# Batch 0 projected head by head into its stacked rows, and the second span's groups spread two to a step, in a one-core language-model layer

## The chip, the cores and the metric

One Trainium2 chip, and of it one core. The time is that of one execution on the device, in microseconds (us), and the number that counts is the median of several executions. All engines of the core run at once: PE (matrix products), DVE (vector work), ACT (activations, copies), POOL (general vector work and, here, the indirect DMAs), and SP, which only issues DMAs. Each engine takes its instructions strictly in order; semaphores tie them together.

## What is computed

Four thousand and ninety-six tokens, in 8 batches of 512, go through three layers. Layer norm and attention are per batch; nothing of one batch's attention depends on another's.

```python
h = einsum('bsd,bsde->bse', base_embeddings[ids], rule_transform[token_rules[ids]])   # D = 64, 100 rules
n = layernorm(h)
q, k = einsum('btd,hrd->bhtr', n, Q), einsum('bud,hrd->bhur', n, K)                  # 8 heads, R = 32
attn = softmax(einsum('bhtr,bhur->bhtu', q, k) / 8)
h = h + einsum('bhtd,hde->bte', einsum('bhtu,bud->bhtd', attn, n), VO)
f = layernorm(h)
y = sum over the top 2 of 8 experts of weight * (relu(f @ W1[e] + b1[e]) @ W2[e] + b2[e])
out = h + y
```

All of it is float32. Products that need the precision are made from two halves, a high part (fp32r) and what is left over (the low part).

## The kernel before

**Spans and groups.** The product of a token with its rule's 64x64 matrix is made after the tokens have been sorted by rule. The tokens are sorted in two spans: span 0 is batches 0 and 1, span 1 is batches 2 to 7. A sorted span is cut into tiles of 64 rows, each of one rule, and 8 tiles are a *group*: 15 groups in span 0, 19 in span 1. For a group PE transposes the input (line 933, tile `eT`), makes 8 pairs of small products with the rule's matrix (line 942), and an engine copies the result to `y_out`, from where a DMA stores it. POOL then gathers each batch's rows back into token order, 4 indirect DMAs per batch (line 450, `hbuf`). The sorting itself (counts by PE, lines 902 and 903; slots by DVE, lines 688 to 701; scatters by POOL, line 442) comes before a span's groups. For groups that are not among the first 100 rules PE must load the rule's column offset from memory into registers first (`columns`).

**Steps.** From batch 0 on the program is one list of steps (b, k), b from -2 to 8 and k from 0 to 15; all engines walk the same list. A step of PE holds, in this order: two transposed score tiles for the exponentials (line 1041, 97 rows: 96 of data and one of maxima), one score tile for the row maxima (line 1057, 96 rows), the product of the exponentials with the values (line 1069, 4 matmuls, "PV"), a list of auxiliary work (`aux_at`), and the other score tile. The maxima (`mx`, line 849) are made on DVE. A *pair* is two score tiles; pair j belongs to PV step j and is scored 12 steps earlier (`LEAD`). The auxiliary work is the projection of later batches, the expert layer of earlier ones, and, until batch 0 ends, the groups of span 1. It takes the two banks 6 and 7 in turn.

**From layer norm to scores.** `xT` transposes a batch's normed rows (`xs`), four projection parts (`proj`, lines 992 and 993) make q and k for all heads, ACT casts them (`qk_h`) and DVE makes the low part (`qk_l`, line 872). Heads lie in the wrong partitions there, so 24 DMAs of 128 KB each copy them into the stacked tiles `qs` and `ks` (lines 385 and 388), six to each of four head pairs. The scores of a head pair wait for its semaphore `stack_g`. The maxima come back as two half rows per batch: PE transposes them (line 1018), ACT negates them (`negm`), SP copies them into row 96 of `qs` (line 394) and waits for the landing. SP also fetches the softmax sums (`srow`, line 405) in the same queue.

**Where things stand in the list.** Span 1's groups stand at (-1,14), (-1,15) and then three to a step from (0,0) on. Batch 2's `xT` is at (0,13), its projection at (0,14) and (0,15); batch 3's `xT` at (1,4) and its projection at (1,5) to (1,8). All 24 gathers of batches 2 to 7 stand in one row on POOL behind the last group's store. Span 1's counts are made by PE between groups 8 and 14 of span 0. Batch 0's key copies go out on ACT's queue, the rest on SP's.

## Time and profile before

| | us |
|---|---|
| three executions | 675.84, 678.07, 680.62; median 678.07 |
| the profiled execution | 675.75, its span 673.9 |
| PE busy | 525.9 (78% of the span) |
| DVE busy | 409.6 (61%) |
| ACT busy | 285.6 (42%) |
| POOL busy | 238.1 (35%) |

The span is the time between the first and the last instruction. "Idle before, releaser" is the time an engine stood, and what let it go on. "Granted clock" is TensorE's: 1.00 is full speed (2.4 GHz), 0.50 is half (1.2 GHz). A wait put down to "remote" or "another core or an unknown queue" is one whose releaser the trace doesn't name.

### The profile page before, as it was taken

Reading aid. Unit: us, or ns where it says so; the run is one execution under the profiler, and the core shown is the slowest. Engines: PE = TensorE matmul, PEld = TensorE weight load, DVE = VectorE, ACT = ScalarE, POOL = GpSimd, SP = SyncE. Lnnn points to the kernel's source line nnn. Section 1 sums busy time; section 2 is a strip of 40 time slices with the busy share of each in tenths; the row PEclk is TensorE's granted clock in tenths of the full one; section 3 lists DMA queues with packets and bytes.
Section 4 is the critical chain, followed back from the end, with each engine's and each line's share of the span. In section 5 each row is a group of like instructions: output and inputs, shape, how many; then the busy total and the mean of one; then the engine's idle time right before and its main releaser. Section 6 shows DMA issues by size and latency. Waiting matters only on the chain.

```text
span 673.9 us, 9098 instructions
## 1 busy us (share of the span) xinstructions
PE 525.9 (78%) x2604; PEld 278.8 (41%) x2604; DVE 409.6 (61%) x970; ACT 285.6 (42%) x548; POOL 238.1 (35%) x395
## 2 busy tenths in 40 slices
PE   0174903797787296999999999999999999988580
PEld 0043802255452133444544544544554454437240
DVE  5621685662225284788868959868857767446521
ACT  0101301055562153546555555565555465652350
POOL 5674057633237500220333224124133232236414
PEclk9985965579998598999999999999999999995976
DMA  8732414722751035440440440431332000000000
GB/s 245 257 89 57 118 36 92 181 62 71 174 141 26 19 78 114 94 96 4 92 96 1 95 103 1 95 79 26 71 79 48 2 9 2 9 1 9 0 9 8
DMA packets 21774, 47.03 MB, mean 70 GB/s; under 512 B 6240, under 2 KB 11552, under 8 KB 21664
## 3 DMA queue, kind: packets, MB, share of 16 engines
q1 hardware_dynamic: 15392, 32.23, 20.2%
q0 software_dynamic: 4752, 8.20, 4.7%
q10 hardware_dynamic: 1584, 6.03, 2.7%
q8 instruction: 24, 0.39, 0.2%
q14 instruction: 22, 0.18, 0.1%
HBM read 9.97 MB, written 11.01 MB: 31 GB/s over the span
## 4 chain that ended last, share of the span: by engine, by line
PE 58%; DVE 16%; issue 10%; ACT 3%; DMA 3%; another core or an unknown queue 3%; POOL 2%; SPq 2%; POOLq 0%; DVEq 0%; ACTq 0%
PE bank L1069 15%; PE bank L1057 10%; PE bank L1041 8%; PE bank L942 6%; PE bank L1027 5%; DVE mx L849 4%; PE bank L1008 4%; PE bank L1002 2%; PE bank L1003 2%; DVE r_sb L867 2%; POOL r_sb L503 2%; DMA front<-in_weights 1%; PE bank L933 1%; PE bank L988 1%
## 5 line engine op out<-in xcount | busy, mean ns | idle before, releaser
L849 DVE TENSOR_REDUCE mx<-bank 128x1 f32<-128x512 f32 x256 | 171.1, 688 | 107.3 <-PE bank L1057 79.0
L503 POOL TENSOR_TENSOR r_sb<-r_sb 128x256 f32<-128x256 f32 (+2 forms) x192 | 99.7, 519 | 287.9 <-DVE r_sb L884 188.1
L560 ACT ACTIVATE prob<-bank 128x512 f32<-128x512 f32 x256 | 138.9, 596 | 68.8 <-PE bank L1041 50.5
L1069 PE MATMUL bank<-prob,xa 128*64 128x512 f32 x512 | 141.5, 631 | 3.6 <-issue 3.6
L1057 PE MATMUL bank<-ks,qs 96*128 96x512 f32 x256 | 123.2, 487 | 25.7 <-DVE mx L849 21.4
L1057 PEld LDWEIGHTS bank<-ks,qs 96*128 96x128 f32 x256 | 50.9, 199 | 144.7 <-issue 122.5
L1041 PE MATMUL bank<-qs,ks 97*128 97x512 f32 x256 | 89.1, 430 | 0.7 <-DMA qs<-negm 0.4
L600 ACT ACTIVATE r_sb<-bank,stay 128x512 f32<-128x512 f32 x64 | 43.1, 687 | 68.3 <-PE bank L1003 68.2
L1041 PEld LDWEIGHTS bank<-qs,ks 97*128 97x128 f32 x256 | 44.0, 195 | 19.4 <-issue 13.0
L942 PE MATMUL bank<-r_sb,eT 128*64 128x64 f32 (+1 forms) x544 | 43.2, 239 | 10.2 <-ACT eT L543 6.8
L942 PEld LDWEIGHTS bank<-r_sb,eT 128*64 128x64 f32 x544 | 38.4, 151 | 17.8 <-issue 9.2
L1069 PEld LDWEIGHTS bank<-prob,xa 128*64 128x64 f32 x512 | 25.7, 137 | 48.5 <-issue 45.7
L450 POOL DMA_INDIRECT hbuf<-y_sorted,pos x32 | 30.6, 957 | 40.1 <-DMA y_sorted<-y_out 31.0
L442 POOL DMA_INDIRECT emb_sorted<-ctxT,pos x32 | 32.7, 1021 | 12.7 <-issue 12.7
L1027 PEld LDWEIGHTS bank<-stay,ctxT 128*128 128x128 f32 x256 | 34.3, 200 | 6.7 <-issue 2.4
L1027 PE MATMUL bank<-stay,ctxT 128*128 128x128 f32 x256 | 36.2, 287 | 0.3 <-DVE r_sb L884 0.3
L434 POOL DMA_INDIRECT ctxT<-in_table,ids x32 | 31.5, 985 | 13.8 <-issue 9.4
L884 DVE TENSOR_TENSOR r_sb<-bank,rsum 128x512 f32<-128x512 f32 x32 | 22.1, 690 | 21.2 <-PE bank L1027 21.0
L1008 PE MATMUL bank<-r_sb,stay 128*64 128x512 f32 x128 | 32.1, 610 | 2.4 <-ACT r_sb L600 2.4
L606 ACT CAST qk_h<-bank 128x512 fp32r<-128x512 f32 x32 | 18.4, 588 | 31.8 <-PE bank L993 24.8
L1002 PE MATMUL bank<-xs,w_h 128*128 128x512 f32 x64 | 30.8, 481 | 1.0 <-DVE r_sb L884 0.5
L872 DVE TENSOR_TENSOR qk_l<-bank,qk_h 128x512 fp32r<-128x512 f32 x32 | 21.7, 687 | 16.2 <-ACT qk_h L606 13.1
(137 smaller groups left out, 603.3 us busy)
## 6 DMA issues: line engine op xcount, KB each, us to landing
qs<-qk_h SPq DMA_DIRECT2D x64, 128.0 KB
ks<-qk_h SPq DMA_DIRECT2D x56, 128.0 KB
qs<-qk_l SPq DMA_DIRECT2D x32, 128.0 KB
ks<-qk_l SPq DMA_DIRECT2D x28, 128.0 KB
emb_sorted<-front ACTq DMA_DIRECT2D x4, 608.0 KB
y_sorted<-y_out POOLq DMA_DIRECT2D x19, 128.0 KB, 2.5
e_in<-emb_sorted POOLq DMA_DIRECT2D x9, 256.0 KB, 3.0
emb_sorted<-front ACTq DMA_DIRECT2D x3, 640.0 KB
```

Source lines behind the costliest of these rows:

```text
L442: nc.gpsimd.indirect_dma_start(emb_sorted[i], bass.IndirectOffsetOnAxis(ap=pos[:, c:c + 1], axis=0), etok[:, c, 0:D], None).then_inc(S[f"s ...
L503: nc.gpsimd.tensor_tensor(a[:, at:at + width], src[:, 0:width], src[:, width:2 * width], ALU.add).then_inc(S["pool_chain"], 1)
L560: nc.scalar.activation(prob[:, step % NPROB, u % 2, :], bank[u % NST][:], ACT.Exp, scale=SC).then_inc(S["exp_done"], 1)
L600: nc.scalar.activation(hid[:, i, :], ring(a)[:], ACT.Relu, bias=b1_f[:, i:i + 1]).then_inc(S["relu_done"], 1)
L849: V.tensor_reduce(mx[:, u // 16, u % 16:u % 16 + 1], bank[3 + n % 2][:], AX.X, ALU.max).then_inc(S["mx_done"], 1)
L942: last = M(out_[0:TS, s * D:(s + 1) * D], eT[:, g % 2, col:col + TS], r_sb[:, at_:at_ + D] if isinstance(at_, int) else r_sb[:, bass.ds(at ...
L1002: M(out_[:], w1_h[:, i * HID:(i + 1) * HID], xs[:, 1, :], start=True, stop=False)
L1008: last = M(out_[64 * t:64 * t + 64, :], w2_f[:, 2 * i + t, :], hid[:, 2 * i + t, :], start=True, stop=True)
L1027: last = M(out_[:, pair * 128:(pair + 1) * 128], ctxT[:, b % 2, pair, i * 128:(i + 1) * 128], vo_blk[:, pair, :, :].rearrange("p t e -> p ...
L1041: M(bank[u % NST][:], ks[:, ub % 2, h, ut * 128:(ut + 1) * 128], qs[:, ub % 2, h, :], start=True, stop=True).then_inc(S["st_ps"], 1)
L1057: M(bank[3 + n % 2][:], qs[0:96, nb % 2, h, tt * 128:(tt + 1) * 128], ks[0:96, nb % 2, h, :], start=True, stop=True).then_inc(S["s_ps"], 1)
L1069: last = M(bank[5][64 * hh:64 * hh + 64, :], xa[:, b % XAR, ut, :], prob[:, (16 * b + k) % NPROB, hh, :], start=(ut == 0), stop=(ut == J - 1))
```

## The change

- **Batch 0 by head.** Its projection no longer goes through `qk_h`, `qk_l` and DMAs. The weights are laid out anew (`wd_h`, `wd_l` in `wide`) so that 16 parts of two 96x512 matmuls each give one head's q or k in stacked form: ACT casts 96 rows straight into `qs` or `ks`, DVE subtracts on 32 rows. The parts stand at steps (-2,10) to (0,0) (`HEAD_AT`), in six banks, since the exponentials' three banks are still unused then. ACT and DVE make the wider weights once, early.
- **Maxima of batch 0 in quarters** (`mq`, `negq`), at steps -3, -1, 1 and 4 counted from (0,0).
- **Pairs** of batch 0 and 1 are scored at steps given by `pair_at`, closer to their use.
- **Span 1's counts** are made after all groups of span 0 (`count(1)`); its slots are made in smaller pieces, and the rule row at step 1.
- **Groups of span 1**: two to a step at (0,4) to (0,13).
- **Batch 1 to 3** are projected at other steps: batch 1 `xT` (0,4) and parts (0,4), (0,5) twice, (0,6); batch 2 `xT` (1,2), parts (1,2), (1,3) twice, (1,4); batch 3 `xT` (1,9), parts (1,10) to (1,13). Batch 1's 24 stack DMAs all go out on SP, behind batch 0's quarter rows.
- **Gathers**: batch 1's go before batch 0's values; batches 2 and 3 (8 in a row) behind the last group, and four more for batch b+3 before `values(b+2)` of each later batch.

```diff
-        R_AT = [(-1, 14), (-1, 15)] + [(0, g // 3) for g in range(18)]
+        RULE_AT = [4 + g // 2 for g in range(NG[1] + 1)]
+        HEAD_AT = [-6, -6, -5, -4, -3, -2, -1, 0]
+        QROW_AT = [-3, -1, 1, 4]
+
+        def pair_at(j):
+
+            if j < 8:
+                return -5 + j // 2
+            return max(j - LEAD, (j - 8) // 2 - 1 if j < 16 else 7 + (j - 16) // 2 if j < 32 else 22 + (j - 32) // 2 if j < 48 else 0)
...
-            return {1: (0, 2), 2: (0, 13)}.get(nb, (nb - 2, XT))
+            return {0: (-2, 4), 1: (0, 4), 2: (1, 2), 3: (1, 9)}.get(nb, (nb - 2, XT))
...
+        early = [a for b in range(-2, 0) for k in range(16) for a in aux_at(b, k) if 16 * b + k < -1]
+        SPARE = (6, 7, 0, 1, 2, 5)
+        home = {a: SPARE[n % len(SPARE)] if n < len(early) else 6 + n % RING for n, a in enumerate(order)}
...
+            sp.wait_ge(S["ones_ok"], 1)
+            ones_row(0)
+            for q in range(4):
+                quarter_row(q)
+            sp.wait_ge(S["trow_ok"], 2)
+            ones_row(1)
+            for g in range(4):
+                stack(1, g)
...
-            for b in range(2, B):
-                bring(1, b)
+            bring(1, 2)
+            bring(1, 3)
...
             for b in range(-2, B + 1):
                 if 2 <= b + 2 < B:
+                    if 4 <= b + 3 < B:
+                        bring(1, b + 3)
                     values(b + 2)
...
+                        if kind == "head":
+                            act.wait_ge(S["hd_ps"], i + 1)
+                            act.wait_ge(S["zeroed_1"], 16 * 4)
+                            stacked = ks if i % 2 else qs
+                            nc.scalar.copy(stacked[0:96, 0, i // 2, :], ring(a)[0:96, :]).then_inc(S["hd_hi"], 1)
...
-            N_AT = {1: (0, 0), 2: (0, 10), 3: (0, 14)}
+            N_AT = {1: (0, 0), 2: (0, 14), 3: (1, 4)}
...
+                        if kind == "head":
+                            dve.wait_ge(S["hd_hi"], i + 1)
+                            low = ks[64:96, 0, i // 2, :] if i % 2 else qs[32:64, 0, i // 2, :]
+                            V.tensor_tensor(low, ring(a)[64:96, :] if i % 2 else ring(a)[32:64, :],
+                                            low.bitcast(F32), ALU.subtract).then_inc(S["hd_lo"], 1)
...
-                if g in (8, 11, 13):
-                    count(1, (8, 11, 13).index(g) + 1)
+            count(1)
...
+                if kind == "head":
+                    pe.wait_ge(S["xs_ready"], 1)
+                    h = i // 2
+                    o = 4 * (2 * (i % 2) + h % 2) + h // 2
+                    M(out_[0:96, :], wd_h[:, o].rearrange("p r n -> p (r n)"), xs[:, 0, :], start=True, stop=False)
+                    last = M(out_[0:96, :], wd_l[:, o].rearrange("p r n -> p (r n)"), xs[:, 0, :], start=False, stop=True)
+                    last.then_inc(S["hd_ps"], 1)
```

Three places, the third on two engines, show how the instructions of an engine stand. A row is the line of its kernel, the operation with its output, its inputs and its shape, and the semaphores that it waits for.

PE from batch 0's first projection to its first scores (`xs` is the transposed batch), before:

```order
L992 MATMUL bank7<-xs,wqk_h 128x512 [waits xs_ready]
L993 MATMUL bank7<-xs,wqk_l 128x512
L992 MATMUL bank6<-xs,wqk_h 128x512 [waits xs_ready]
L993 MATMUL bank6<-xs,wqk_l 128x512
L992 MATMUL bank7<-xs,wqk_h 128x512 [waits xs_ready,qk_lo]
L993 MATMUL bank7<-xs,wqk_l 128x512
L992 MATMUL bank6<-xs,wqk_h 128x512 [waits xs_ready,qk_lo]
L993 MATMUL bank6<-xs,wqk_l 128x512
L910 MATMUL bank5<-cst,trule 1x128 [waits trule_ok]
L1057 MATMUL bank3<-ks,qs 128x512 [waits stack_0]
L1057 MATMUL bank4<-ks,qs 128x512 [waits stack_0]
L1057 MATMUL bank3<-ks,qs 128x512 [waits mx_done,stack_0]
```

The same place after the change:

```order
L1082 MATMUL bank7<-xs,wide 96x512 [waits xs_ready]
L1083 MATMUL bank7<-xs,wide 96x512
L1082 MATMUL bank0<-xs,wide 96x512 [waits xs_ready]
L1083 MATMUL bank0<-xs,wide 96x512
L1082 MATMUL bank1<-xs,wide 96x512 [waits xs_ready]
L1083 MATMUL bank1<-xs,wide 96x512
L1082 MATMUL bank2<-xs,wide 96x512 [waits xs_ready]
L1083 MATMUL bank2<-xs,wide 96x512
L1175 MATMUL bank3<-ks,qs 128x512 [waits hd_lo]
L1175 MATMUL bank4<-ks,qs 128x512 [waits hd_lo]
L1082 MATMUL bank5<-xs,wide 96x512 [waits xs_ready]
L1083 MATMUL bank5<-xs,wide 96x512
```

The four parts before the rule row are now sixteen narrower ones, of which four stand ahead of the first scores, and the scores wait for `hd_lo` in place of `stack_0`.

POOL at the end of span 1's groups, before (`y_sorted1` is span 1's stored output, `pos` the rows to gather):

```order
L333 DMA e_in<-emb_sorted1 128x256 [waits eT_ps]
L338 DMA y_sorted1<-y_out 64x2x256 [waits y_ok] x7
L450 DMA hbuf<-y_sorted1,pos 128x64 [waits y_out1_0,y_out1_1,y_out1_3,y_out1_2]
L450 DMA hbuf<-y_sorted1,pos 128x64 x23
L458 COPY xa<-xn 128x4x63 [waits xn_ready]
L458 COPY xa<-xn 128x4x63 [waits pv_done,xn_ready]
```

After:

```order
L371 DMA y_sorted1<-y_out 64x2x256 [waits y_ok] x7
L497 DMA hbuf<-y_sorted1,pos 128x64 [waits y_out1_0,y_out1_1,y_out1_3,y_out1_2]
L497 DMA hbuf<-y_sorted1,pos 128x64 x7
L505 COPY xa<-xn 128x4x63 [waits xn_ready]
L497 DMA hbuf<-y_sorted1,pos 128x64 x4
L505 COPY xa<-xn 128x4x63 [waits pv_done,xn_ready]
```

The row of 24 gathers is a row of 8, and four more follow each later batch.

SP at the end of batch 0 and the start of batch 1, after the change (lines 425 and 428 are the stack copies, 434 the half rows of maxima):

```order
L434 DMA qs<-negm 1x16x128 [waits negm_ready]
L425 DMA qs<-qk_h 32x1024 [waits exp_done,qk_lo,m_in]
L425 DMA qs<-qk_l 32x1024
L425 DMA qs<-qk_h 32x1024
L428 DMA ks<-qk_h 32x1024 x2
L428 DMA ks<-qk_l 32x1024
L425 DMA qs<-qk_h 32x1024 [waits exp_done]
L425 DMA qs<-qk_l 32x1024
L425 DMA qs<-qk_h 32x1024
L428 DMA ks<-qk_h 32x1024 x2
L428 DMA ks<-qk_l 32x1024
L434 DMA qs<-negm 1x16x128 [waits negm_ready]
```

Before, the second half row of batch 1 (the first `negm` row here) also stood behind batch 2's last six copies; the half row that ends this piece is batch 2's first, and it stands behind twelve of batch 3's copies as it did before, while batch 3's projection, for which they wait, has moved from (1,5) to (1,8) to (1,10) to (1,13).

PE at (1,13) to (1,15), after, where that half row is made (line 1128) and batch 3's last projection part stands right before it:

```order
L1102 MATMUL bank7<-xs,wqk_h 128x512 [waits xs_ready,vo_used]
L1103 MATMUL bank7<-xs,wqk_l 128x512
L1128 MATMUL bank6<-cst,mx 16x128 [waits mx_done,qk_lo]
L1137 MATMUL bank7<-stay,ctxT 128x128 [waits ctx_copied,qk_lo]
L1137 MATMUL bank7<-stay,ctxT 128x128 x3
L1158 MATMUL bank2<-qs,ks 128x512 [waits exp_done,ks_one,m_in]
L1158 MATMUL bank0<-qs,ks 128x512 [waits exp_done,ks_one,m_in]
L1175 MATMUL bank3<-ks,qs 128x512 [waits mx_done,stack_2]
L1188 MATMUL bank5<-prob,xa 64x512 [waits xa_ready,exp_done]
L1188 MATMUL bank5<-prob,xa 64x512
```

Two steps on, at (1,15), the matmuls of line 1158 that prepare (2,0) are the first that need this half row in `qs` (`m_in`).

## Rows read from the trace of the kernel before

**Rows 1.** The page: busy time of PE; PE's granted clock in 40 slices.

```profile
PE 525.9 (78%) x2604; PEld 278.8 (41%) x2604; DVE 409.6 (61%) x970; ACT 285.6 (42%) x548; POOL 238.1 (35%) x395
...
PEclk9985965579998598999999999999999999995976
```

**Rows 2.** Windows of core 0: start:end us, busy us of each engine (x instructions), clock.

```profile
130.00:140.00 10.00, 8.80 (x16) 4.37 (x17) 6.90 (x11) 1.51 (x5) 6.32 (x8) 0.50 0.40 119
...
220.00:234.00 14.00, 3.05 (x6) 0.87 (x6) 1.90 (x3) 0.00 (x0) 7.77 (x9) 0.50 0.10 21
...
340.00:380.00 40.00, 38.63 (x171) 18.62 (x169) 32.51 (x76) 22.81 (x43) 10.65 (x24) 1.00 0.25 56
```

**Rows 3.** Timeline, first span's end to batch 0's scores: start, us, engine, line, operation, idle.

```profile
91.69 0.99 DVE L688 TENSOR_TENSOR sel<-oh,cnt 128x800 f32<-128x800 bf16 x1
...
96.50 0.42 DVE L753 TENSOR_REDUCE ln_s<-hbuf 128x4 f32<-128x256 f32 x1
...
104.49 0.80 PE L992 MATMUL bank<-xs,wqk_h 128*128 128x512 f32 x1 [1.40 <-DVE xs L855]
...
110.57 0.53 SPq L385 DMA_DIRECT2D qs<-qk_h  x1
...
117.42 1.22 PE L1057 MATMUL bank<-ks,qs 96*128 96x512 f32 x2 [0.50 <-DMA ks<-qk_l]
...
133.28 0.77 PE L1057 MATMUL bank<-ks,qs 96*128 96x512 f32 x1 [0.28 <-DVE mx L849]
```

**Rows 4.** Timeline, steps of batch 0, with groups and, from 199 us, bare.

```profile
150.94 1.08 PE L1069 MATMUL bank<-prob,xa 128*64 128x512 f32 x4
...
158.20 1.08 PE L1069 MATMUL bank<-prob,xa 128*64 128x512 f32 x4
...
163.74 0.44 PE L933 MATMUL bank<-cst,e_in 128*128 128x128 f32 x2 [0.94 <-DVE qk_l L872]
...
199.35 1.08 PE L1069 MATMUL bank<-prob,xa 128*64 128x512 f32 x4
...
201.50 1.08 PE L1069 MATMUL bank<-prob,xa 128*64 128x512 f32 x4
```

**Rows 5.** Timeline, last group store to batch 2's layernorm.

```profile
197.29 0.61 POOL L338 DMA_DIRECT2D y_sorted<-y_out  x1 [0.47 <-ACT y_out L580]
...
200.38 1.02 POOL L450 DMA_INDIRECT hbuf<-y_sorted,pos  x1 [2.48 <-DMA y_sorted<-y_out]
...
206.64 0.42 DVE L753 TENSOR_REDUCE ln_s<-hbuf 128x4 f32<-128x256 f32 x1 [0.75 <-DMA hbuf<-y_sorted,pos]
```

**Rows 6.** Timeline, batch 2's stack copies and what waits behind them.

```profile
242.28 0.40 PE L992 MATMUL bank<-xs,wqk_h 128*128 128x512 f32 x1
...
245.09 0.53 SPq L385 DMA_DIRECT2D qs<-qk_h  x1
...
263.19 0.59 SPq L394 DMA_DIRECT2D qs<-negm  x1
...
266.94 1.22 PE L1041 MATMUL bank<-qs,ks 97*128 97x512 f32 x2
...
274.17 0.40 PE L992 MATMUL bank<-xs,wqk_h 128*128 128x512 f32 x1
...
276.21 0.51 SPq L385 DMA_DIRECT2D qs<-qk_h  x1
```

**Rows 7.** Waits of the whole span: engine, tile, line, releaser: us, times, longest.

```profile
DVE mx L849 <- remote: 18.6, 4, 10.5
...
ACT prob L560 <- remote: 17.0, 2, 14.8
```

**Rows 8.** The chain of waits: start us, us, what it went through.

```profile
222.33 10.43 another core or an unknown queue
```

**Rows 9.** Waits in the window 49 to 63 us, columns as in rows 7.

```profile
ACT eT L543 <- remote: 6.8, 1, 6.8
```

**Rows 10.** DMA issues: tile, queue, count, size, us to landing.

```profile
qs<-negm SPq DMA_DIRECT2D x16, 8.0 KB, 1.8
```

More of the change, by code:

```diff
@@ L243, in aux_at @@
                 todo.append(("down", b - 3, 3))
-            if k == MT[1] and 0 <= b < B:
+            if k == MT[1] and 1 <= b < B:
                 todo.append(("mt", b, 1))
@@ L262, in aux_at @@
                 todo += [("down", b - 2, p) for p in range(3) if DOWN[p] == k]
-            for g in range(TOTAL - BASE[1] + 1):
-                if R_AT[g] == (b, k):
+            at_ = 16 * b + k
+            todo += [("mq", 0, q) for q in range(4) if QROW_AT[q] == at_]
+            todo += [("head", 0, 2 * h + t) for h in range(H) if HEAD_AT[h] == at_ for t in range(2)]
+            todo += [("row", 1, 0)] if at_ == 1 else []
+            for g, rule_step in enumerate(RULE_AT):
+                if rule_step == at_:
                     todo += [("rT", BASE[1] + g, 0)] if g < NG[1] else []
@@ L316, in s_units @@
         def s_units(b, k):
-            nb, kk = divmod(16 * b + k + LEAD, 16)
-            return [(nb, 2 * kk), (nb, 2 * kk + 1)] if 0 <= nb < B else []
+            return [divmod(2 * j + t, 32) for j in range(16 * B) if pair_at(j) == 16 * b + k for t in range(2)]
         gate_exps = [(b + 2, 15) for b in range(B - 2)] + [(B, 5), (B, 14)]
@@ L326, in lm_tower_kernel, with span_of @@
         ys = [t.rearrange("(g h m s) d -> g m h (s d)", h=2, m=TS, s=4) for t in y_sorted]
+        def span_of(g):
+            return sum(g >= base for base in BASE) - 1
         def load_pair(eng, n):
-            i = n >= NP0
+            i = span_of(PAIRS[n][0])
             g, at_ = PAIRS[n][0] - BASE[i], 2 * n % NE_IN
@@ L680, in starts, with slots @@
                 link(V.tensor_tensor(first, ends, more, ALU.subtract))
[L681 to L685 removed]
+                link(V.scalar_tensor_tensor(key, first, float(B * T), cum[:, 0:NR], ALU.mult, ALU.add))
+            def slots(i, quarters, known):
                 lo = SPAN[i][0]
[L687 to L690 removed]
+                p0, p1 = quarters[0] * QC, (quarters[-1] + 1) * QC
+                both, nth, ahead, at_in, past, gap, tile_, hi, mid, low, two = (slot_i[:, j, 0:p1 - p0] for j in range(11))
+                for q in quarters:
+                    c = q * QC - lo
+                    link(V.tensor_tensor(sel[:], oh[:, c:c + QC, :], key.unsqueeze(1).to_broadcast([128, QC, NR]), ALU.mult))
+                    link(V.tensor_reduce(slot_f[:, c:c + QC], sel[:], AX.X, ALU.add))
+                    yield
+                link(V.tensor_tensor(both, slot_f[:, p0 - lo:p1 - lo], rank[:, p0:p1], ALU.add))
                 link(V.tensor_scalar(nth, both, SHIFT, (B * T >> SHIFT) - 1, ALU.logical_shift_right, ALU.bitwise_and))
@@ L736, in _ @@
                 V.tensor_copy(y_out[:, g % 4, :], bank[2 + g % 2][0:TS, :]).then_inc(S["y_ok"], 1)
-                if 5 <= g < 9 or g >= 11:
-                    next(later, None)
+                if g >= 8:
+                    next(later)
             run(later)
-            starts(1)
-            slots(1, 1)
-            slots(1, 2)
+            starts(1, bank[4], bank[5])
+            run(slots(1, (1,), 2))
+            later = slots(1, (2, 3), 3)
+            next(later)
             def layernorm(b, done):
@@ L827, in _ @@
                 for k in range(16):
-                    if (b, k) == (-2, 9):
-                        slots(1, 3)
+                    if (b, k) in ((-2, 0), (-1, 0), (-1, 11)):
+                        next(later)
+                    if (b, k) == (0, 0):
                         tile_rules(1)
@@ L834, in _ @@
                     norms += [layernorm(nb, "xn_ready") for nb in range(1, B) if N_AT.get(nb, (nb - 3, 8)) == (b, k)]
-                    for _ in range((4 if k < 3 else 2) if b == 0 else 1):
+                    for _ in range(2 if b == 0 or b == 1 and k < 14 else 1):
                         while norms and next(norms[0], norms) is norms:
@@ L954, in _ @@
                 M(bank[6][:, 0:384], ident, cst[:, 0:384], start=True, stop=True)
+            for g in range(NR // GT, NG[0]):
+                columns(g)
             for g in range(NG[0] + 1):
                 if g < NG[0]:
-                    columns(g)
+                    if g not in tile_at:
+                        columns(g)
                     if g >= 2:
@@ L979, in aux @@
                 drained(pe, a)
+                if kind == "head":
+                    pe.wait_ge(S["xs_ready"], 1)
[4 more added lines that the diff above has]
+                    last.then_inc(S["hd_ps"], 1)
+                if kind == "mq":
+                    pe.wait_ge(S["mx_done"], 8 * (i + 1))
+                    nc.tensor.transpose(out_[0:2 * J, 0:128], mx[:, i // 2, i % 2 * 2 * J:(i % 2 + 1) * 2 * J], ident).then_inc(S["mq_ps"], 1)
+                if kind == "row":
+                    rule_row(1, out_)
                 if kind == "rT":
```

322 lines of the change are left out of this document (181 added, 141 removed).

## Prediction

> **What bounds the kernel now.** I read the page first. PE is busy 525.9 us of 673.9, and its granted clock is near full from the 15th slice on [rows 1]. The windows say where PE's idle time lies: in 340 to 380 it is busy 38.63 us of 40 at clock 1.00, so from there to the end the kernel is bound by PE, and a batch costs what its matmuls cost. The change alters nothing in that part. In 130 to 140, where batch 0 is scored, PE is busy 8.80 us of 10, but at clock 0.50; in 220 to 234 it is busy 3.05 us of 14 [rows 2]. So what can be won or lost lies between the end of the first span (85 us) and the point where the steady batches begin. I take as that point the exponential matmuls of step (1,7), at 266.94 [rows 6], and ask when the changed kernel gets there and what is left to do behind it.
>
> The timeline shows how 85 to 267 is spent: a serial run of handoffs to batch 0's projection at 104.49, stack copies from 110.57, first scores at 117.42 [rows 3], slow steps with groups (7.26 us from 150.94 to 158.20, against 2.15 for a bare one) [rows 4], and from about 209 to 234 a hole in which PE, ACT and DVE all stand: nearly all of DVE's 18.6 us and ACT's 17.0 us of waits whose releaser is not named lie there [rows 7], and 10.43 us of the chain goes through it in one piece [rows 8]. In that hole POOL runs its 24 gathers, begun at 200.38 [rows 5], and little else. Then batch 2's projection ends at 242.28, SP's copies run from 245.09, and (1,7) waits for the half row issued at 263.19, 18.10 us after the first of 24 copies and two fetches [rows 6].
>
> **Part by part.** Sums are against the profiled execution, 675.75 us, which is 2.3 below the median of 678.07.
>
> *Slots.* Before batch 0's layer norm DVE makes two quarters of slots, the second from 91.69 until the layer norm at 96.50 [rows 3]. After, only the product and the sum of the second, 2 us of these 4.8, stand there; with the counts' rest this gives **-3.0**, so `xs` is ready at 101.5 instead of 104.49.
>
> *Heads in place of copies.* The 6.85 us from the first copy to the first score [rows 3], and the 6 us of projection ahead, go. In their place come 16 parts of two matmuls. Such a pair takes PE 1.3 to 1.4 us at the low clock (0.80 for one, pipelined) [rows 3]; ACT's cast and DVE's subtract run beside it, about 0.7 each, and bind no more than PE does. Four parts: DVE is done at about 106.6, and a slot piece makes it 107.6. Step -5 with one pair of score tiles (0.77 to 0.80 a tile at the low clock [rows 3]) and two parts: 3.9. Four steps of the same kind with handoffs: 5.0 each (4.1 at full clock). Steps 0 to 3 with exponentials, quarter rows and pairs: 19.1 at the low clock, 16.5 at full. Start of step (0,4): 144.4 to 150.6; I take **148**, nearer the low clock, since the clock in 130 to 140 was 0.50 even with PE 88% busy [rows 2]. The wider weights cost ACT and DVE some 3.5 us, before 52 us, where both wait for data: nothing.
>
> *Groups two to a step.* A group costs (7.26 - 2.15)/3 = 1.7 us of a step [rows 4]; I take 1.8, and 2.3 where columns are loaded from memory (groups 12 to 18). A step with two groups is then 6.1, with loaded columns 6.8. Steps 4 to 6 hold batch 1's transpose and projection as well, which before made PE wait 0.94 us at 163.74 for the subtract [rows 4]: 8.05, 7.1, 6.2. Step 7 begins batch 1's scores, whose copies have by then just begun to land: 9.3 (3.3 of it waiting). Steps 8 to 13: 6.1, 6.1, three of 6.8, 5.9. Sum 69.3: step (0,14) starts at **217.3**.
>
> *Gathers.* Batch 2's layer norm needs the last group's store (197.29), then 3.1 us to the first gather and 6.26 to the layer norm at 206.64 [rows 5]. After, the last store is near 218.0, so the layer norm starts at **227.7**, 21.1 later than before; at (0,14) DVE waits for it and PE behind DVE, 8 us. The 24 gathers become 8 and then fours. Does the hole return? A burst of 24 gathers shows such waits, and so does one of 14 (6.8 us of ACT in 49 to 63 [rows 9]). I take zero for eight, and 5 us as the other bound, about the wait that the 14 caused.
>
> The Trainium skill, page "SBUF — State Buffer", section "Who interferes with whom", says that DMA never contends with a compute engine and that PE and ACT never wait on anyone. The trace speaks against reading that as no effect of any kind: ACT stood 17.0 us with no named releaser while gathers were all that ran [rows 7]. By the page the hole is not the gathers' and would come again, which is a rival below.
>
> *Projection 2 to (1,7).* The layer norm and two-chunk steps, then transpose and four parts at (1,2) to (1,4): last part at 247.6, against 242.28. From there the same road as before: 2.0 us to SP (274.17 to 276.21 shows it), 18.1 to the half row, 1.8 to land [rows 6, 10], and (1,7)'s exponentials at **269.7** against 266.94: **+2.8**. PE stalls some 16 us in (1,5) and (1,6), since batch 2's copies come behind its projection, and the half row of batch 1 behind them all.
>
> *What is left behind (1,7).* Two score tiles, and batch 3's projection, of which parts stood before (1,7) and now stand at (1,9) to (1,13): **+1.9** of PE time.
>
> *A new wait at (1,15).* Batch 3's last part now stands at (1,13) and batch 2's first half row behind twelve of batch 3's copies: 2.0 + 12 x 0.65 (18.1 us for 26 transfers with a wait between [rows 6]) + 1.8 = 11.4 from the last part to the exponentials of (2,0). PE has 4.4 us of work before it must wait: **+7.0**. Before, that part was at 274.17 and (1,15) far behind. What is queued on SP behind the half row are stack copies needed later still; who waits is PE, and with it ACT.
>
> *Clock.* After two stalls of that size the trace shows the granted clock down at 0.50 (in 220 to 234 [rows 2]); work at half speed for a few us: **+2**.
>
> Sum: 2.8 + 1.9 + 7.0 + 2.0 = **+13.7**: 689.5 profiled, 691 to 692 as a median. The removed hole is inside this sum, since all was built forward from 85 us: it is worth some 20 us, and the groups ending at 217 instead of 197, and the later copies, take it back.
>
> **Rivals.** *Only the hole goes, and handoffs hide (same).* If the group steps run at 1.4 a group and the clock in the head stage is mostly full, step (0,14) starts near 206, 11 us earlier than in the forecast, and all behind it moves with it, while the new wait and its clock stay: 677 to 684. It decides from a start of (0,14) before 210 on. For it: a whole step of three groups took 7.26 us with full clock [rows 4], handoffs included, and with two there is more bare work to cover each. Chance 0.18.
>
> *Faster.* PE-bound throughout: head stage at full clock (144.4), 19 groups at 1.39, no wait at step 7: step (0,14) at 195.5, batch 2's layer norm near 206, (1,7) near 247, 20 earlier; +7, +2 and +1.9 remain: 666 to 672. It decides from a start of (0,14) before 197 on, since the forecast's 13.7 and the 6.8 of a measurable gain make 20.5 us from 217.3. For it: in 340 to 380 PE stands for 1.4 us of 40 only [rows 2], so handoffs can be covered. Against it: in the group steps of before they were not, a group taking 1.7 us where its matmuls take less, and the clock at batch 0's scores was 0.50. Chance 0.17.
>
> *Eight gathers still disturb.* +5, about 697. Chance 0.08.
>
> *The hole is not the gathers'* and comes again near the layer norms: +20, about 712. Chance 0.07. This is what the page's rule would give.
>
> *The wait at (1,15) isn't there* because the half row is made earlier or PE has more cover: 691 - 9 = 682 to 684; within the forecast's range. The rest, 0.50, is the forecast with its bounds: the head stage 144.4 to 150.6, groups 1.7 to 2.3, waits at (1,15) 3 to 9: 683 to 702.
>
> **Numbers.** A measurement of this kernel can tell about 1% (6.8 us) from no change. Slower by over 1% (above 684.9): most of the forecast and both disturbed rivals, 0.62. Within 1%: 0.22, the same rival and the low edge of the forecast. Faster: 0.16. To hold eight in ten the range reaches from 668, which leaves out a part of the faster rival, to 703, which leaves out the return of the hole.
>
> **What would show it.** Right: the first score of batch 0 near 105 and step (0,4) near 148; no waits without a named releaser beyond a few us; batch 2's layer norm at 222 to 230; a wait of PE of 5 to 9 us at (1,15) released by the exponentials' half row. Wrong: step (0,14) before 206, or copies that are done before PE needs them; a hole again behind the last group.

## The result and the profile after

The changed kernel takes 709.93 us in the median of four executions (705.2 to 713.68), the kernel before 679.35 beside it (675.84 to 683.3): 1.0445 times as long, 95% interval 1.0357 to 1.0533. The forecast was 691 in a range of 668 to 703, slower with a chance of 0.62. The direction came out as forecast, the size did not: +30.6 us where +13 were expected.

The profiled execution after took 709.02 us, span 707.2. The page, its busy times and PE's granted clock, as in [rows 1]:

```profile
PE 539.7 (76%) x2630; PEld 286.5 (41%) x2630; DVE 418.4 (59%) x971; ACT 294.7 (42%) x563; POOL 240.3 (34%) x395
...
PEclk9985957699899685798999999999999999997976
```

PE has 13.8 us more busy time, part of it work at half clock; the rest of the 33.3 us is PE standing. Windows of the changed kernel, columns as in [rows 2]:

```profile
119.00:130.00 11.00, 1.79 (x5) 0.88 (x3) 2.06 (x3) 1.43 (x3) 8.20 (x9) 0.50 0.08 24
...
228.00:241.00 13.00, 3.48 (x11) 1.27 (x12) 3.13 (x8) 2.00 (x4) 8.14 (x9) 0.76 0.19 38
...
262.00:284.00 22.00, 7.13 (x20) 2.61 (x18) 7.04 (x21) 2.33 (x6) 0.39 (x1) 0.58 0.64 146
...
310.00:328.00 18.00, 10.54 (x45) 5.29 (x41) 6.26 (x11) 4.35 (x9) 7.88 (x13) 0.81 0.59 138
...
340.00:380.00 40.00, 39.45 (x181) 20.23 (x179) 31.74 (x80) 23.78 (x45) 12.11 (x21) 1.00 0.31 71
```

In 340 to 380 the kernel is bound by PE as before. The first four windows are where it is not: PE is busy 1.79 us of 11, 3.48 of 13, 7.13 of 22, 10.54 of 18, and the clock is 0.50 to 0.81. Where the PV step (b, k) starts tells where time is lost (both traces, us):

| PV step | before | after | difference |
|---|---|---|---|
| (0,0) | 143.7 | 141.4 | -2.3 |
| (0,4) | 180.8 | 156.4 | -24.4 (groups still ahead) |
| (0,14) | 236.7 | 228.2 | -8.5 |
| (1,0) | 243.8 | 244.3 | +0.5 |
| (1,6) | 259.1 | 269.1 | +10.0 |
| (1,7) | 268.5 | 285.1 | +16.6 |
| (2,0) | 294.7 | 328.0 | +33.3 |
| end of the span | 673.9 | 707.2 | +33.3 |

All of the loss is made before (2,0). The timeline of the head stage, which answers to [rows 3]:

```profile
102.26 0.74 PE L1082 MATMUL bank<-xs,wide 128*96 128x512 f32 x1 [1.47 <-DVE xs L950]
...
119.36 1.05 PE L1175 MATMUL bank<-ks,qs 96*128 96x512 f32 x2
...
123.86 0.58 ACT L632 CAST qs<-bank 96x512 fp32r<-96x512 f32 x1 [3.24 <-remote]
...
127.37 0.58 ACT L632 CAST ks<-bank 96x512 fp32r<-96x512 f32 x1 [2.93 <-remote]
...
129.62 0.77 PE L1175 MATMUL bank<-ks,qs 96*128 96x512 f32 x1 [9.21 <-issue]
```

The first head part starts at 102.26, 2.2 us earlier than the first part before. But between 119.4 and 129.6 nearly nothing happens: the score tile issued at 119.36 is the last for 9 us, and ACT's casts start 3.5 us apart, though the matmuls whose results they take had been issued by 118.93. The waits whose releaser isn't named:

```profile
DVE y_out L815 <- remote: 23.5, 2, 12.8
...
ACT srow L635 <- remote: 4.8, 1, 4.8
...
ACT qs L632 <- remote: 3.2, 1, 3.2
...
ACT ks L632 <- remote: 2.9, 1, 2.9
```

The first lies in the first span's groups (ended at 51.8 and 63.1), the last three between 115 and 128 us. The hole that the kernel before had at 209 to 234 [rows 7, 8] is gone. The road of batches 2 and 3, which answers to [rows 5, 6]:

```profile
237.70 0.42 DVE L833 TENSOR_REDUCE ln_s<-hbuf 128x4 f32<-128x256 f32 x1 [12.51 <-DMA hbuf<-y_sorted,pos]
...
239.66 0.77 PE L1175 MATMUL bank<-ks,qs 96*128 96x512 f32 x1 [9.52 <-DVE mx L934]
...
261.00 0.40 PE L1103 MATMUL bank<-xs,wqk_l 128*128 128x512 f32 x1
...
262.88 0.51 SPq L425 DMA_DIRECT2D qs<-qk_h  x1
...
268.42 0.79 PE L1175 MATMUL bank<-ks,qs 96*128 96x512 f32 x1 [4.86 <-DMA ks<-qk_l]
...
277.24 0.56 PE L1132 MATMUL bank<-cst,srow 8*128 8x8 f32 x4 [5.40 <-DMA srow<-ctxT]
...
281.58 0.59 SPq L434 DMA_DIRECT2D qs<-negm  x1
...
283.57 1.22 PE L1158 MATMUL bank<-qs,ks 97*128 97x512 f32 x2 [4.62 <-DMA qs<-negm]
...
310.84 0.40 PE L1102 MATMUL bank<-xs,wqk_h 128*128 128x512 f32 x1
...
312.88 0.51 SPq L425 DMA_DIRECT2D qs<-qk_h  x1
...
320.41 0.60 SPq L434 DMA_DIRECT2D qs<-negm  x1
...
323.22 1.22 PE L1158 MATMUL bank<-qs,ks 97*128 97x512 f32 x2 [6.17 <-DMA qs<-negm]
```

The reader is to see five waits in turn: DVE's for the gathers, which ends at 237.70 and holds PE for 9.52 us; PE's for batch 2's first copies (4.86), for the sums (5.40), for batch 1's half row (4.62), and at (1,15) for batch 2's half row, issued at 320.41 behind twelve copies (6.17). They make 30.6 us together.

### The profile page after: what moved, and what is told of

Same layout as the page of the kernel before. It is cut to its first block, busy times and chain, and to the rows that moved or that the text cites. A ratio compares the mean times of both kernels' runs of the same rounds, so it can differ in the third digit from the quotient of the medians.

```text
span 707.2 us, 9133 instructions
## 1 busy us (share of the span) xinstructions
PE 539.7 (76%) x2630; PEld 286.5 (41%) x2630; DVE 418.4 (59%) x971; ACT 294.7 (42%) x563; POOL 240.3 (34%) x395
## 4 chain that ended last, share of the span: by engine, by line
PE 58%; DVE 14%; issue 9%; DMA 5%; POOL 4%; SPq 4%; ACT 4%; another core or an unknown queue 1%; POOLq 0%; DVEq 0%; ACTq 0%
PE bank L1188 16%; PE bank L1175 10%; PE bank L1158 7%; PE bank L1038 5%; PE bank L1137 4%; PE bank L1118 4%; DVE mx L934 3%; PE bank L1112 2%; PE bank L1113 2%; SPq L425 2%; SPq L428 2%; DVE r_sb L962 2%; POOL r_sb L548 1%; PE bank L1029 1%; DMA front<-in_weights 1%
## 5 line engine op out<-in xcount | busy, mean ns | idle before, releaser
L1188 PE MATMUL bank<-prob,xa 128*64 128x512 f32 x512 | 145.6, 648 | 0.0
L1158 PE MATMUL bank<-qs,ks 97*128 97x512 f32 x256 | 91.4, 439 | 12.0 <-DMA qs<-negm 12.0
L1158 PEld LDWEIGHTS bank<-qs,ks 97*128 97x128 f32 x256 | 45.7, 201 | 31.6 <-issue 13.0
L1038 PE MATMUL bank<-r_sb,eT 128*64 128x64 f32 (+1 forms) x544 | 44.0, 242 | 11.4 <-ACT eT L596 6.1
L1038 PEld LDWEIGHTS bank<-r_sb,eT 128*64 128x64 f32 x544 | 39.2, 154 | 19.2 <-DVE y_out L815 6.4
L497 POOL DMA_INDIRECT hbuf<-y_sorted,pos x32 | 31.5, 984 | 37.4 <-DMA y_sorted<-y_out 28.7
L371 POOL DMA_DIRECT2D y_sorted<-y_out x19 | 11.6, 612 | 78.7 <-ACT y_out L627 78.5
L1112 PE MATMUL bank<-xs,w_h 128*128 128x512 f32 x64 | 30.7, 480 | 1.2 <-DVE r_sb L979 0.7
L967 DVE TENSOR_TENSOR qk_l<-bank,qk_h 128x512 fp32r<-128x512 f32 x28 | 19.1, 688 | 20.9 <-ACT qk_h L663 20.9
```

What stands on the lines that cost most here:

```text
L1038: last = M(out_[0:TS, s * D:(s + 1) * D], eT[:, g % 2, col:col + TS], r_sb[:, at_:at_ + D] if isinstance(at_, int) else r_sb[:, bass.ds(at ...
L1112: M(out_[:], w1_h[:, i * HID:(i + 1) * HID], xs[:, 1, :], start=True, stop=False)
L1158: M(bank[u % NST][:], ks[:, ub % 2, h, ut * 128:(ut + 1) * 128], qs[:, ub % 2, h, :], start=True, stop=True).then_inc(S["st_ps"], 1)
L1188: last = M(bank[5][64 * hh:64 * hh + 64, :], xa[:, b % XAR, ut, :], prob[:, (16 * b + k) % NPROB, hh, :], start=(ut == 0), stop=(ut == J - 1))
```

## Experiments

Ratios are to the kernel before on the same chip, and that kernel took different times on different chips: 641 to 642 us on chips 6 and 11, 679 to 684 on chips 0, 1, 13 and in the first measurement. The table has all runs; their edits and expectations follow.

| run | chip | median us | ratio (95%) |
|---|---|---|---|
| before_same | 11 | 641.75 | 0.9991 (0.9958 to 1.0025) |
| after_same | 11 | 691.92 | 1.0760 (1.0637 to 1.0883) |
| a_row15 | 6 | 679.98 | 1.0582 (1.0499 to 1.0666) |
| a_rows | 6 | 667.55 | 1.0395 (1.0341 to 1.0449) |
| a_g3 | 11 | 684.98 | 1.0638 (1.0560 to 1.0716) |
| a_rows_g3 | 0 | 690.11 | 1.0113 (1.0028 to 1.0198) |
| a_gath24 | 11 | 690.99 | 1.0740 (1.0660 to 1.0820) |
| a_gath24b | 13 | 730.92 | 1.0695 (1.0642 to 1.0748) |
| a_scat | 6 | 698.29 | 1.0915 (1.0846 to 1.0985) |
| a_scat2 | 13 | 713.24 | 1.0464 (1.0398 to 1.0530) |
| a_sched | 0 | 680.35 | 0.9998 (0.9959 to 1.0037) |
| a_sched2 | 13 | 686.49 | 1.0018 (0.9977 to 1.0060) |
| a_sched3 | 1 | 680.30 | 1.0006 (0.9975 to 1.0037) |
| a_sched_rows | 0 | 690.73 | 1.0139 (1.0072 to 1.0206) |
| b_row7 | 0 | 685.26 | 1.0116 (1.0046 to 1.0185) |
| b_split | 6 | 641.40 | 1.0004 (0.9976 to 1.0032) |
| b_split2 | 13 | 668.23 | 0.9769 (0.9723 to 0.9815) |
| b_pace | 1 | 657.36 | 0.9653 (0.9611 to 0.9695) |

### Both kernels again (before_same, after_same)

No edit.

> The kernel before the change, unchanged, profiled beside its changed form on one chip. The run with the split gathers took 641.4 us where the kernel before took 641.35 beside it, with PE never standing at 190 to 215 us. Theory (the hole of 25 us is not the gathers'): the profile of this run shows the 24 gathers in one row and no hole behind the last group; span 636 to 642. Rival (the gathers make the hole and the split form lost as much elsewhere): a hole of 10 us or more at 190 to 220 us.

> The changed kernel, unchanged, beside its former form on one chip. With no hole to remove there, the change should cost more than the 30 us of the first measurement: 686 to 692, since the run with the half row of (1,15) moved took 680.0. Rival (the row brought nothing): 678 to 682.

The kernel before, windows of that run behind the last group, where POOL gathers (182 to 212 us):

```profile
190.00:199.00 9.00, 7.39 (x29) 3.23 (x30) 8.21 (x23) 3.55 (x8) 6.87 (x8) 1.00 0.15 26
...
199.00:209.00 10.00, 9.07 (x34) 3.94 (x32) 9.23 (x23) 7.10 (x15) 7.56 (x9) 1.00 0.18 35
```

Both expectations held, the second at the edge of its range (686 to 692). The 24 gathers stand in one row, and PE is busy 7.39 of 9 and 9.07 of 10 us at clock 1.00, where it was busy 3.05 of 14 in [rows 2]. No wait of this run is put down to an unnamed releaser. So on this chip there is no hole to remove, and the change costs 7.6%. PE's long waits in the changed kernel there:

```profile
218.34 0.77 PE L1175 MATMUL bank<-ks,qs 96*128 96x512 f32 x1 [9.62 <-DVE mx L934]
...
244.11 0.79 PE L1175 MATMUL bank<-ks,qs 96*128 96x512 f32 x1 [4.88 <-DMA ks<-qk_l]
...
252.90 0.56 PE L1132 MATMUL bank<-cst,srow 8*128 8x8 f32 x4 [5.37 <-DMA srow<-ctxT]
...
259.06 1.22 PE L1158 MATMUL bank<-qs,ks 97*128 97x512 f32 x2 [4.44 <-DMA qs<-negm]
...
296.91 1.22 PE L1158 MATMUL bank<-qs,ks 97*128 97x512 f32 x2 [6.10 <-DMA qs<-negm]
```

They are those of the first chip, to a few tenths: 9.62, 4.88, 5.37, 4.44 and 6.10 us, 30.4 together. Against before_same, (0,0) starts 6.5 us earlier, (0,14) 7.3 later, (1,6) 23.2 later, (2,0) 44.9 later.

### SP's order (a_row15, a_rows)

```diff
+                if b == 1:
+                    max_row(2, 0)
                 if 0 <= b + 2 < B:
                     stack(b + 2, 0)
```

> The changed kernel with one change of order on SP: batch 2's first half row of maxima goes out ahead of batch 3's first twelve stack copies. Theory 1 (batch 1 is starved by its queue of copies: PE waits 6.2 us at (1,15) for this row and runs at half clock for some us behind it): 6 to 9 us faster than the changed kernel's 709, so 700 to 703. Rival (PE would wait there anyway, for batch 3's copies or the maxima): within 2 us of 709.

> As before it, and the sums' fetch of batch 0 ahead of all copies of batch 2 and batch 1's second half row behind the first six copies instead of behind all 24. Theory 1: the waits of 5.4 us (sums) and 4.6 us (half row) at (1,6) and (1,7) go too, with some half clock behind them, while the copies are 2 to 3 us later: 9 to 12 us faster than the run with the (1,15) row alone, 690 to 693. Rival (the projection of batch 2 is late and the copies themselves set the pace): 0 to 4 us faster only, 697 to 702.

a_rows has, besides, for b = 0 the order sums of batch 0, stack(2, 0), max_row(1, 1), stack(2, 1), stack(2, 2). Both went the way of theory 1. From 1.076 (chip 11) to 1.058 (chip 6) is some 12 us, more than the 6 to 9 expected, but this compares two chips, and the intervals of the two runs leave anything from 2 to 21. The traces are tighter: from PV step (1,7) to (2,0) a_row15 takes 31.4 us (266.5 to 297.9), after_same 41.1 and a_gath24 40.8, so taking out one wait of 6.1 (there 5.5) us gave 9 to 10. From 1.058 to 1.040 on one chip is another 12, at the upper end of what was expected. A 4 to 6 us wait of PE thus costs more than its length. The trace after shows why: behind the wait of 9.52 us three PV steps take 3.9 us each (240.4, 244.3, 248.2, 252.0) at clock 0.50, against 2.15 in a bare one [rows 4]. How long that lasts differs: behind the same wait (9.62) after_same's three steps take 3.65, 2.90 and 2.15 us (from 219.0), a_gath24's 3.9 each.

### Groups three to a step (a_g3, a_rows_g3)

```diff
-        RULE_AT = [4 + g // 2 for g in range(NG[1] + 1)]
+        RULE_AT = [4 + g // 3 for g in range(NG[1] + 1)]
```

> The changed kernel with span 1's groups three to a step instead of two, (0,4) to (0,10). Theory 1 (the late end of the groups and the gathers behind them make PE stand 9.5 us at (0,14)): that wait goes, with the half clock behind it: 8 to 13 us faster than the changed kernel on the same chip. Rival (the groups themselves cost the same and the later waits for batch 2's copies take what is won, since its projection stays at (1,2) to (1,4)): within 3 us.

> The changed kernel with both half rows and the sums moved ahead on SP, and the groups three to a step. If the two gains add, they give 24 + 7 us: ratio to the kernel before 1.03 or a little less. Rival (they overlap, as both end in the wait for batch 2's copies): 1.04, as with the rows alone.

a_g3 gave 7 us of 692, a little under the 8 to 13 expected, and the intervals (1.056 to 1.072 against 1.064 to 1.088) overlap, so it isn't clear of noise. In the trace (0,14) to (0,15) shrank from 12.3 to 6.6 us, but (1,7) was only 3.0 us earlier. a_rows_g3 ran on another kind of chip, with the first measurement's 1.0445 as the nearest reference: 3.3% or 23 us. Whether the two gains add stays open, since no chip had both.

### The former places, the new head stage (a_sched, a_sched2, a_sched3)

```diff
-        RULE_AT = [4 + g // 2 for g in range(NG[1] + 1)]
+        RULE_AT = [g // 3 for g in range(NG[1] + 1)]
...
-            return {0: (-2, 4), 1: (0, 4), 2: (1, 2), 3: (1, 9)}.get(nb, (nb - 2, XT))
+            return {0: (-2, 4), 1: (0, 3), 2: (0, 13)}.get(nb, (nb - 2, XT))
...
-            N_AT = {1: (0, 0), 2: (0, 14), 3: (1, 4)}
+            N_AT = {1: (0, 0), 2: (0, 10), 3: (0, 14)}
```

> The changed kernel with the second half of the change taken back: span 1's groups three to a step from (0,0), batch 1 projected at (0,3) to (0,5), batches 2 and 3 where they stood before ((0,13) to (0,15) and (1,4) to (1,8)), layer norms too; batch 0 by head, quarter rows and split gathers stay. Theory 1 (the loss is made by the places of the projections and groups, not by the head stage): on a chip where the kernel before takes 642 it takes 634 to 646. Rival (the head stage, its quarter rows and SP's later batch 1 copies carry the loss): above 665.

> The changed kernel with the former places of groups and projections, once more: it took as long as the kernel before on a chip of the second kind, with a standstill of 13 us in its head stage. On a chip of the first kind the head stage alone is left to tell: its PV step (0,0) starts 6 to 7 us earlier, ratio 0.98 to 1.00 (theory: the head stage gains, its group steps give part of it back), or 1.00 to 1.02 (rival: the group steps, slower by quarter rows, scores and batch 1's copies in them, give back more). On a chip of the second kind again 1.00.

> The changed kernel with the former places of groups and projections, a third time, in the hope of a chip without standstills: there the head stage alone is left to tell, ratio 0.98 to 1.00 if it gains and 1.00 to 1.02 if its slower group steps give back more. On a chip with standstills: 1.00 again.

Three times 1.00 (0.9998 to 1.0018), all on chips with standstills. Taking the places of groups, projections and layer norms back takes the whole loss of 4.5% back. But a_sched has split gathers too, which alone give 0.977 on such a chip (below): if the two add, the head stage with its group steps costs those 2.3%. In a_sched the first six steps take 66 us (141.2 to 207.6) against 53.5 before, and its head stage has waits of 3.6 and 8.6 us without a named releaser. So the theory's 634 to 646 us on a chip without standstills stayed untested: none of the three ran on one.

### Rows ahead of copies in the former order (a_sched_rows, b_row7)

b_row7 is the kernel before with SP's order stack(2, 0), sums, stack(2, 1), max_row(1, 1), stack(2, 2).

> The same, with batch 0's sums fetched ahead of batch 2's copies and batch 1's second half row behind the first six of them. Theory: PE's wait at (1,7) (9.3 us between the products of (1,6) and (1,7) against 2.2 in a bare step) shrinks by 4 to 7 us: that much faster than the run without. Rival (the copies themselves are the wait): within 2 us.

> The kernel before the change, with SP's order changed at the same place: batch 0's sums behind batch 2's first six copies, batch 1's second half row behind the first twelve. Theory: its own wait at (1,7) goes: 4 to 7 us faster than the kernel before. Rival (copies, not rows): within 2 us.

Both came out slower, by 10 and 5 us: neither theory nor rival. The timeline of b_row7 at (1,6):

```profile
260.10 0.52 SPq L394 DMA_DIRECT2D qs<-negm  x1
...
272.82 0.59 PE L1029 MATMUL bank<-cst,srow 8*128 8x8 f32 x4 [9.98 <-DVE qk_l L879]
```

the same wait in the kernel before:

```profile
266.43 0.59 PE L1022 MATMUL bank<-cst,srow 8*128 8x8 f32 x4 [5.30 <-DVE qk_l L872]
```

and in a_sched, without the reordering:

```profile
264.39 0.59 PE L1132 MATMUL bank<-cst,srow 8*128 8x8 f32 x4 [4.62 <-DVE qk_l L967]
```

PE waits for DVE's `qk_l` of batch 3's projection, and that for ACT's cast, which may not overwrite `qk_h` until all of batch 2's 24 copies have left it. SP held the last twelve copies back until the half row was ready at 260.10, so this wait is 9.98 us there, against 5.30 before; in a_sched_rows, which is a_sched with SP's order of a_rows for batch 0's sums and batch 1's second half row, it is 15.93, against 4.62 in a_sched. So in the kernel before PE's last wait ahead of (1,7) was for these copies, and not for the half row, as the prediction read [rows 6]: the row had been issued at 263.19, and moving it forward could win nothing. With batch 3's projection at (1,5) to (1,8) the copies come first; with it at (1,10) to (1,13), as in the changed kernel, the rows do.

### Long rows of indirect DMAs (b_split, b_split2, a_gath24, a_gath24b)

```diff
-            for b in range(2, B):
-                bring(1, b)
+            bring(1, 2)
+            bring(1, 3)
...
+                    if 4 <= b + 3 < B:
+                        bring(1, b + 3)
                     values(b + 2)
```

This makes b_split from the kernel before; a_gath24 is the changed kernel with the same lines taken back.

> The kernel before the change, with one part of the change alone: behind the last group's store POOL gathers batches 2 and 3 only, and four more for each later batch in its turn. Theory 2 (the hole at 209 to 234 us goes with the row of 24 gathers): the hole shrinks by 10 us or more, 655 to 668. Rival (the hole has another source): within 3 us of 676.

> The changed kernel with all 24 gathers of batches 2 to 7 in one row behind the last group again. If gathers make PE's results late: 10 us or more slower than the changed kernel on the same chip. If they don't: within 2 us.

> The former kernel with the gathers split, once more, since chips differ: on two of them no engine stands for a releaser that the trace doesn't name, on two others all kernels do, and there the hole at 209 to 234 us was seen with 24 gathers in one row and not with 8. On a chip of the second kind, theory 2 (a long burst of indirect DMAs makes PE's results late there): no hole behind the last group, ratio 0.965 to 0.98. Rival (the hole follows the stretch at full clock ahead of it, whatever POOL does): the hole stays, ratio 0.995 to 1.005. On a chip of the first kind both give 1.00.

> The changed kernel with its 24 gathers in one row, once more. On a chip of the second kind, theory 2: a hole of 10 us or more behind the last group, ratio 1.06 or more, against 1.0445 for the changed kernel. Rival: no hole, 1.04 to 1.05. On a chip of the first kind: 1.074 as before.

On chips 6 and 11, where there is no hole to remove, the gathers' order changes nothing (1.0004; 1.074 against 1.076). On chip 13 it is worth 2.3% in the old kernel and, against the first measurement's 1.0445, 2.5% in the new; both are inside what was expected. The traces give the hole alone: in the old kernel 31.5 us from (0,11) to (0,15) (209.0 to 240.5) against 12.7 in b_split2, so 19; in the new one 39.2 us from (1,0) to (1,6) in a_gath24b against 24.9 in the changed kernel, so 14. Windows of b_split2 behind the last group:

```profile
210.00:220.00 10.00, 8.07 (x29) 3.06 (x30) 7.42 (x17) 4.54 (x9) 5.71 (x6) 1.00 0.13 23
...
220.00:234.00 14.00, 13.06 (x52) 5.91 (x48) 12.68 (x33) 7.99 (x17) 4.24 (x5) 1.00 0.06 11
```

No hole. And in a_gath24b the timeline shows one again, where the changed kernel has none (start, us, engine, tile, idle before):

```profile
267.60 0.69 DVE L932 TENSOR_REDUCE mx<-bank 128x1 f32<-128x512 f32 x1 [8.52 <-remote]
...
269.00 0.60 ACT L605 ACTIVATE prob<-bank 128x512 f32<-128x512 f32 x1 [12.13 <-remote]
```

POOL began its 24 gathers there at 239.54.

### The scatters held back (a_scat, a_scat2)

```diff
+            pool.wait_ge(S["hd_lo"], 2 * H)
             place(1, range(2 * J + QC, NC), 3)
```

> The changed kernel, with POOL's last 16 scatters of the second span held back until the head projection of batch 0 is through. Theory 2 (PE's results come late while POOL issues a long burst of indirect DMAs, as between 119 and 130 us): the standstill in the head stage goes, the head parts end near 125, and a standstill may come in the steps behind it, where the scatters now run; the total moves by -5 to +5. Rival (the standstill comes from PE itself, when the clock falls or rises in this stage): it stays at its place with no indirect DMA under way, and the groups start later by some 10 us: +5 to +12.

> The changed kernel with its last 16 scatters held back until the head parts are through, once more. On a chip of the second kind, theory 2: no standstill in the head stage, step (0,0) some 10 us earlier than the changed kernel's 141 us there, and a standstill later, where the scatters run. Rival: a standstill of 9 to 13 us in the head stage as in the changed kernel, with no indirect DMA under way. On a chip of the first kind: ratio 1.09 as before.

As a change it costs: 1.5% more than the changed kernel on chips without standstills, since the groups' input lands later (in a_scat PE waits 10.63 us for it, between (0,4) and (0,5)). There was no standstill to move, so a_scat tells nothing of its two theories. As a test a_scat2 decides. Its windows in the head stage, with no indirect DMA under way, and where the scatters then ran (138 to 158 us):

```profile
112.00:125.00 13.00, 9.96 (x24) 5.95 (x25) 9.76 (x16) 3.18 (x6) 0.00 (x0) 0.63 0.00 0
...
146.00:160.00 14.00, 5.53 (x17) 1.91 (x16) 3.22 (x6) 2.79 (x5) 9.78 (x11) 0.87 0.08 26
```

```profile
152.39 0.58 ACT L616 COPY ctxT<-bank 128x512 f32<-128x512 f32 x1 [5.38 <-remote]
...
155.18 0.69 DVE L935 TENSOR_REDUCE mx<-bank 128x1 f32<-128x512 f32 x1 [6.62 <-remote]
```

The head stage has no standstill: from the first head part to PV step (0,0) it takes 29.9 us (102.3 to 132.2), where a_gath24b on the same chip takes 44.4 (103.3 to 147.6), the changed kernel in the first measurement 39.1, and on chip 11 29.7. The other traces fall in line: with all scatters in that stage it takes 39.4 to 45.2 us on chips 0 and 13 (a_sched, a_sched_rows, a_rows_g3, a_sched2) and 29.8 to 30.6 on chips 6 and 11 (a_gath24, a_row15, a_g3). The clock rose and fell in a_scat2's head stage too (a mean of 0.63 from 112 to 125), so its changes alone don't make the standstill. The waits without a named releaser have moved with the scatters.

### The fetches let go in fours (b_pace)

```diff
-            fetch(range(FIRST + 10, NC))
+            for n, c in enumerate(range(FIRST + 10, NC, 4)):
+                if n:
+                    pool.wait_ge(S["y_ok"], 2 * n)
+                fetch(range(c, min(c + 4, NC)))
```

> The former kernel with the gathers behind the last group split, and the 14 table fetches of the second span, which start at 42 us in one row, let go four at a time, the next four after two more groups of the first span. On a chip with standstills, theory 2: the one between 47 and 62 us goes or shrinks too, ratio 0.95 to 0.965 against 0.977 with the gathers alone split. Rival (that standstill belongs to PE's start at full clock, not to the fetches): 0.975 to 0.98. On a chip without standstills: 1.00.

b_pace has the lines of b_split besides.

The chain of waits of b_split2, and below it that of b_pace, in the first groups:

```profile
47.02 9.99 another core or an unknown queue
...
57.05 4.16 another core or an unknown queue
```

```profile
55.35 6.56 another core or an unknown queue
```

14.2 us shrank to 6.6. It didn't go: by the time of the second pause two more groups were through, and eight fetches ran from 50.28 in one row; the standstill begins 5 us into them. At 0.9653, at the upper edge of what was expected, this is the lowest ratio measured, against 1.0445 for the changed kernel and 1 for the one before. What the pacing adds to the split is less sure than the ratios of two chips make it (0.9653 against 0.9769): PV step (0,0) starts at 143.8 us here, at 148.3 in b_split2 and at 143.7 in the kernel before. On a chip without standstills it wasn't run.

## Why the prediction was right or wrong

**Slots and start of the heads.** -3.0 forecast, 102.26 instead of 104.49 measured: -2.2, so 0.8 short.

**Heads in place of copies: the step that failed first.** (0,4) was forecast at 148, within 144.4 to 150.6, and came at 156.4. The term priced the head parts by PE's matmuls and the handoffs, and took the standstills for a matter of the gathers behind the last group. POOL issues 32 indirect DMAs from 87.31 to 129.6 in the same stage, and from 119.4 to 129.6 PE stands. I asked whether eight gathers would still disturb, and not what else runs beside the new head stage. With 16 of the scatters out of the way (a_scat2) the stage to (0,0) is as short as on a chip without standstills, 29.9 us instead of 39.1; the term's own steps give 26.4 to 30.0 (from 101.5 to between 127.9 and 131.5). So the prices of the parts were right, and the standstill was the term put at nothing. The four steps behind it took 15.0 us where 16.5 to 19.1 were forecast, which hid some of the miss. The kernel before, in which PE waited for stack copies there (110 to 117 [rows 3]), had less to lose: from its first projection matmul to (0,0) it takes 39.2 us in the first measurement and 36.5 on chip 11. Its row of 28 indirect DMAs, which starts at 88.7, ran on past 117.42, when PE scored, and from 85 to 145 no wait without a named releaser is longer than 0.7 us: such a row alone is not enough to bring a standstill.

**Groups two to a step.** 69.3 forecast, 71.8 measured on the first chip and 72.1 on chip 11 (134.6 to 206.7). 4% low, and that close partly by luck: steps 4 to 7, with batch 1's projection and the wait for its copies, took 37.4 us instead of 30.7, and steps 8 to 13 took 34.4 instead of 38.5. The steps priced at 6.8, for loaded columns, took 5.5. (The terms as written add up to 69.2, and a step at 2.15 + 2 x 1.8 is 5.75, not 6.1.)

**Gathers and layer norm.** From the last store's end to the layer norm 9.7 us were forecast (218.0 to 227.7), 9.5 measured (228.2 to 237.7). The 9.52 us wait of PE was forecast at 8. That 8 gathers don't bring the hole back held, and the price of the removed hole, some 20 us, was nearly right: 19 by the traces of the old kernel. The Trainium skill, page "SBUF — State Buffer", section "Who interferes with whom", which is about the ports of that memory, says that DMA never contends with a compute engine and that PE and ACT never wait on anyone. On chips 0, 1 and 13 waits of 5 to 12 us come and go with rows of indirect DMAs, so here the measurement decides against reading that as no effect of any kind, while chips 6 and 11 agree with it. What in those rows holds PE's results back, POOL's issuing or the transfers themselves, isn't shown.

**Projection 2 to (1,7).** Last part forecast at 247.6, measured 261.0: 10 of the 13.4 us were carried over, 3.4 were new. (1,7)'s exponentials 269.7 forecast, 283.57 measured; 22.1 against 22.6 us from the last part. The number is right, the road not quite the same: before, PE's last wait ahead of (1,7) was for `qk_l` and the copies (5.30), after it was for the half row (4.62).

**The new wait at (1,15).** +7.0 forecast, 6.17 measured, behind 12 copies as described. Right. (2.0 + 12 x 0.65 + 1.8 is 11.6, not 11.4.)

**Clock: the other term that failed.** It was put at +2, for all. From (1,7)'s exponentials to the PV step (2,0) 38.7 us were forecast (27.8 before, and 10.9), 44.4 measured, at a mean granted clock of 0.78 where the same road had 0.91 before. Of the 3.4 us ahead of batch 2's last part most are the three steps at 3.9 us: on chip 11, where the clock came back sooner, (0,15) to (1,3) takes 13.5 us instead of 16.5. That is some 9 us on top of the 2. That they are the clock's is worked out from these rows; no run held the clock. a_row15 shows the size: taking one wait of 6.1 us out gave 9 to 10 in the trace.

The sum closes: 8.4 (heads, 0.8 of it from the slots) + 2.5 (groups) + 3.0 (to (1,7)) + 5.7 (behind it) = 19.6, and 689.5 + 19.6 = 709.1 against 709.0.

**Rivals.** "Faster" and "same" rested on (0,14) before 197 or 210; it started at 228.2. "Eight gathers still disturb" and "the hole is not the gathers'" were both wrong in their mechanism, though the last named a time, 712, that came near. The forecast's picture of the waits behind (0,14) was right, and of the clock behind them only the size was off; the standstill in the head stage was not in it.

## What to carry to other kernels

When a stage is filled with PE work that used to wait, list what the other engines issue beside it: rows of indirect DMAs that cost little before may now lie on the path. Price a wait of PE at its length plus the half-clock steps behind it, read from a stretch like it, and give that a range. And in an in-order DMA queue ask of each transfer which buffer it frees as well as who reads it: the right place of a short row ahead of a long row of copies depends on whether the copies' source is the next thing waited for.

## What the runs showed of the hardware

- Chips differ by 6% for one kernel: 641 to 642 us on two, 679 to 684 on the others. A large part of it are standstills in which ACT and DVE take up matmuls 5 us or more after PE's record has them, while POOL issues indirect DMAs in long rows (14 to 24; in b_pace also 8 soon after 4). With the rows spread out the kernel before takes 2.3% less (24 gathers, chip 13) and 3.5% less (with the 14 fetches, chip 1), and on the other two chips the gathers' split changes nothing. Why some chips do this isn't known, nor why some such rows bring no standstill.
- A comparison across chips is worth little: the change costs 4.5% on one and 7.6% on another. In the traces the kernel before has a hole of 19 us on the first that the change takes away, and the changed kernel 9 us more in its head stage there.
- After PE stood for 9.5 us its steps ran at the 1.2 GHz level for 12 us, 3.9 us each instead of 2.15; in after_same, after 9.6 us, only the first two were longer (3.65 and 2.90).
